# A two-layer graph network on one core: preparation in another order, and the edge network's first layer as one float32 product

## The chip, the cores and the metric

The kernel runs on one core of a Trainium2 chip. The metric is the device time of one execution in microseconds, as a median of several. Engines are named as in the profile: PE is TensorE (matmul) and PEld its weight load, DVE is VectorE, ACT ScalarE, POOL GpSimd, and SP SyncE, which only issues DMAs here.

## What is computed

The graph has 6250 nodes with 256 features and 100,000 edges sorted by target `dst`, each with 64 attributes. The reference, cut to what matters:

```python
h = relu(layernorm(x))
e = relu(edge_attr @ ee_w1 + ee_b1) @ ee_w2 + ee_b2        # edge network, 64 -> 256 -> 256
agg = segment_sum(h[src] + e, dst)                          # and a self edge for each node
h1 = (1 + eps) * h + agg
h1 = relu(ln(h1 @ w1 + b1)); h1 = relu(ln(h1 @ w2 + b2))    # 256 -> 1024 -> 1024
x = x + relu(ln(h + h1 @ w3 + b3))                          # 1024 -> 256
# then a graph attention layer (8 heads) over the same edges, added to x
```

## The kernel before

It runs in five stages, with a barrier between them.

**Preparation** (`prepare`). The nodes are 50 tiles of 125, taken in ten groups `c` of five. For a group, SyncE loads x; VectorE takes the statistics (`stats`: L315, L318 into `mv`); ScalarE takes the root (`deviation`, L241); VectorE makes the scale and offset (`coefficients`: L323, L324, the latter a product of `mv` and `rstd` on five columns); ScalarE normalises (L247); GpSimd adds a bias (L224, into `ht`) and clears half of the accumulator (L226); ScalarE rounds `ht` to float16 (`high`, L255) and VectorE subtracts to get the rest (`low`, L334); TensorE transposes both parts (L301, L302, into `own_ps`), and ScalarE and VectorE copy the transposed halves out (`own`, L261 and L329). Float32 values are kept throughout as a float16 high part and a float16 low part. The rows go to a table in DRAM. Besides, the kernel works out factors (`own_factors`), an offset by a small product (`own_offset`), and from `dst` a schedule of node tiles for each block of edges (`extremes`, `schedule`). Each engine has its own queue, written out in the loops over `c`; engines meet by semaphores.

**First edge stage** (`edges0`). 196 blocks of 512 edges. Per block GpSimd issues four indirect DMAs (L529), called gathers below, each of which fetches the table rows of 128 edges into `rows`, a ring of six blocks. SyncE loads the block's attributes, twice, into the two halves of `ea` (L493, L494). ScalarE rounds them to float16 (`high_parts`: `eab` L539, `eah` L540), VectorE subtracts for the low part (`low_parts`, L635). TensorE multiplies with the first-layer weights, which are split too: two float16 products for each of the four chunks of 128 edges (L583, L584). ScalarE takes the relu as high part (`rh`, L561), VectorE the low part (`rl`, L667). TensorE then sums rows and edge values by target with a one-hot matrix (`hot`, L407, made by VectorE): 32 products (L597, L598) for the block, and 32 more where it crosses into another tile. VectorE adds the sums to the accumulator (L644, L657). Twelve times in the stage a row of the dense weights is split as well (VectorE L719, L728). The ring is released by VectorE (L648).

**Dense stage** (`nodes`). The 50 tiles go through three layers in a software pipeline; `high_h` (ScalarE, L1120) and `low_h` (VectorE, L1183) split the next tile's input, `deviation(0)` and `inverse(0)` serve the first layer's normalisation.

**Second edge stage and end** (`edges1`, `finish`) do the attention over the same edges, with gathers of their own (L1538) and a float32 product for the sums (L1604).

Of the kernel before, what the change touches and what calls it, by code (L numbers as in the profile page):

```python
# [32 lines left out]
P = 128  # L33
# [23 lines left out]
def build(nc, t, out):  # L57

    with ExitStack() as ctx:
# [18 lines left out]
        with ExitStack() as first:  # L78
# [33 lines left out]
def prepare(nc, t, dram, sb):  # L112


    with ExitStack() as ctx:
# [20 lines left out]
        er = m.sb("er", [P, D], F32)  # L136
        ebr = m.sb("ebr", [ED + 2, D], F32)
        ebh = m.sb("ebh", [ED + 2, D], F16)
        stat = m.sb("stat", [TN, NT, 6], F32)
        mv = m.sb("mv", [TN, NT, 2], F32)  # L140
# [9 lines left out]
        own_ps = [[m.ps(f"own{s}{j}_ps", [P, 8, P]) for j in range(KD)] for s in range(2)]  # L150
        off_ps = own_ps[1][1][:, 7, 0:KD]
# [6 lines left out]
        eb_high, eb_split, ewb_done = m.sem("eb_high"), m.sem("eb_split"), m.sem("ewb_done")  # L158
# [19 lines left out]
        def _(sp):  # L178
# [4 lines left out]
            load_x(0)  # L183
            sp.dma_start(w2e[:], t["L0_gnn_ee_w2"].rearrange("(k p) n -> p k n", p=P)).then_inc(ld_w2e, 16)
            load_x(1)
            sp.dma_start(drow[:], t["dst_flat"].rearrange("(p j e) -> p j e", p=half, j=2)).then_inc(ld_dst, 16)
            for c in range(2, CH):
                load_x(c)
            sp.dma_start(sb["srcs"][:], t["src_cols"]).then_inc(stored, 16)
# [22 lines left out]
        def _(pool):  # L212
# [5 lines left out]
            pool.dma_start(sb["dsts"][:], t["dst_cols"]).then_inc(cols_in, 16)  # L218
            pool.wait_ge(ld_b2, 16)
            for c in range(CH):  # L220
# [5 lines left out]
                pool.memset(acc[:, tiles(c), D:2 * D], 0.0)  # L226
# [3 lines left out]
        def _(act):  # L230
# [3 lines left out]
            act.dma_start(er[0:ED, :], t["L0_gnn_ee_w1"]).then_inc(ld_small, 16)  # L234
            act.dma_start(er[ED:2 * ED, :], t["L0_gnn_ee_w1"]).then_inc(ld_small, 16)
            act.dma_start(ebr[0:ED, :], t["L0_gnn_ee_w1"]).then_inc(ld_small, 16)
            act.dma_start(ebr[ED:ED + 2, :], t["L0_gnn_ee_b1"].partition_broadcast(2)).then_inc(ld_small, 16)
# [19 lines left out]
            def own(c):  # L257
# [3 lines left out]
                act.activation(accT[:, tiles(c), 0, 0:TN], own_ps[c % 2][0][:, 0:PG, 0:TN], ACT.Identity,  # L261
                               bias=own_off[:, 0:1], scale=eps2[:]).then_inc(own_kept[0], 1)

            act.wait_ge(consts, 1)
            deviation(0)
            for c in range(CH + 3):
                if c < CH:
                    normalised(c)
                if c + 1 < CH:
                    deviation(c + 1)  # L270
                if c == 0:
                    act.wait_ge(ld_small, 16 * 4)
                    act.activation(sb["ewa"][:], er[:], ACT.Copy)
                    act.activation(ebh[:], ebr[:], ACT.Copy).then_inc(eb_high, 1)
# [4 lines left out]
                if c == 4:  # L279
                    act.wait_ge(eb_split, 1)  # L280
                    act.dma_start(sb["ewb"][ED:ED + 1, :], ebh[ED:ED + 1, :]).then_inc(ewb_done, 16)
            act.wait_ge(ewb_done, 16)

        @block.tensor
        def _(pe):
# [20 lines left out]
        def _(dve):  # L306
# [20 lines left out]
            def own(c):  # L327
                dve.wait_ge(own_done, c + 1)
                dve.tensor_scalar(accT[:, tiles(c), 1, 0:TN], own_ps[c % 2][1][:, 0:PG, 0:TN], eps2[:], own_off[:, 1:2],  # L329
# [46 lines left out]
            for c in range(CH + 3):  # L376
                if c < CH:
                    coefficients(c)
                if c + 1 < CH:
                    stats(c + 1)  # L380
# [1614 lines left out]
```

## Time and profile before

| | |
|---|---|
| median of 3 runs | 3149.57 us (3146.88 to 3150.08) |
| the profiled execution | 3146.9 us, span 3144.7 us |
| busy share of the span | PE 78%, PEld 69%, DVE 70%, ACT 47%, POOL 64% |
| DMA | 374.02 MB, mean 119 GB/s |

The shares are averages over stages that differ, so they don't say what bounds the kernel; the rows below are taken by stage. A matmul's duration includes the way through the array, so matmuls that follow each other overlap in the rows: how often they start says more than how long one is.

### The profile page before, as it was taken

Reading aid. Unit: us, or ns where it says so; the run is one execution under the profiler, and the core shown is the slowest. Engines: PE = TensorE matmul, PEld = TensorE weight load, DVE = VectorE, ACT = ScalarE, POOL = GpSimd, SP = SyncE. Lnnn points to the kernel's source line nnn. Section 1 sums busy time; section 2 is a strip of 40 time slices with the busy share of each in tenths; the row PEclk is TensorE's granted clock in tenths of the full one; section 3 lists DMA queues with packets and bytes.
Section 4 is the critical chain, followed back from the end, with each engine's and each line's share of the span. In section 5 each row is a group of like instructions: output and inputs, shape, how many; then the busy total and the mean of one; then the engine's idle time right before and its main releaser. Section 6 shows DMA issues by size and latency. Waiting matters only on the chain. (4 is left out here: it accounts for less than half of the span.)

```text
span 3144.7 us, 87336 instructions
## 1 busy us (share of the span) xinstructions
PE 2451.4 (78%) x29338; PEld 2168.6 (69%) x29339; DVE 2188.8 (70%) x3937; ACT 1481.8 (47%) x3763; POOL 2001.7 (64%) x2102
## 2 busy tenths in 40 slices
PE   2677777777777769999999999947777777777773
PEld 1566666666666669999999999935555555655552
DVE  7676667777676737777777777657667667666767
ACT  5444444444444448888888888831111111111114
POOL 4677777777777724444444444437777777777772
PEclk9998889999989989999999999979888878897886
DMA  6555555555555510000000000026555555555554
GB/s 157 167 159 150 157 158 160 162 162 162 160 162 158 152 29 20 20 21 20 23 20 21 20 23 20 21 73 176 172 168 173 173 173 168 172 173 174 171 168 139
DMA packets 184258, 374.02 MB, mean 119 GB/s; under 512 B 42757, under 2 KB 94103, under 8 KB 184184
## 3 DMA queue, kind: packets, MB, share of 16 engines
q0 software_dynamic: 75552, 209.66, 23.5%
q1 hardware_dynamic: 107664, 162.63, 17.3%
q10 hardware_dynamic: 968, 0.87, 0.1%
q8 instruction: 31, 0.51, 0.1%
q14 instruction: 43, 0.35, 0.0%
HBM read 347.21 MB, written 25.80 MB: 119 GB/s over the span
## 5 line engine op out<-in xcount | busy, mean ns | idle before, releaser
L529 POOL DMA_INDIRECT rows<-tab_scratch,srcs x784 | 770.5, 983 | 238.7 <-issue 234.4
L1538 POOL DMA_INDIRECT a_rows<-tab_scratch,srcs x784 | 751.6, 959 | 250.9 <-issue 232.2
L1604 PE MATMUL sum_ps<-feat,a_hot 128*125 128x264 f32 x1960 | 609.6, 468 | 229.5 <-DVE feat L1696 122.2
L1604 PEld LDWEIGHTS sum_ps<-feat,a_hot 128*125 128x125 f32 x1960 | 422.9, 225 | 335.5 <-DVE feat L1696 134.2
L951 PE MATMUL z_ps<-ah,w 128*128 128x125 f16 x6400 | 555.8, 219 | 0.7 <-PEq L1048 0.7
L951 PE MATMUL z_ps<-al,w 128*128 128x125 f16 x3200 | 544.8, 218 | 0.0
L951 PEld LDWEIGHTS z_ps<-ah,w 128*128 128x128 f16 x6400 | 491.5, 97 | 1.3 <-issue 1.3
L1548 ACT ACTIVATE feat<-d 128x32 f32<-128x32 f32 x196 | 44.9, 229 | 827.5 <-DVE d L1692 582.8
L597 PE MATMUL sum_ps<-hot,rows 128*128 128x125 f16 x1960 | 355.9, 235 | 41.9 <-DMA rows<-tab_scratch,srcs 20.9
L583 PE MATMUL mlp_ps<-ewa,eab 128*128 128x256 f16 x788 | 211.0, 298 | 226.8 <-PEq L579 222.3
L561 ACT ACTIVATE rh<-mlp_ps 128x1024 f16<-128x1024 f32 x196 | 199.6, 1018 | 346.4 <-ACTq L560 340.4
L914 POOL TENSOR_TENSOR a<-a 128x500 f32<-128x500 f32 x100 | 149.3, 1493 | 327.9 <-POOLq L913 327.9
L597 PE MATMUL sum_ps<-hot,rh 128*128 128x125 f16 x1960 | 353.9, 234 | 0.0
L598 PE MATMUL sum_ps<-hot,rows 128*128 128x125 f16 x1960 | 353.6, 234 | 0.0
L598 PE MATMUL sum_ps<-hot,rl 128*128 128x125 f16 x1960 | 353.5, 234 | 0.0
L1109 ACT ACTIVATE a<-z,pack 128x125 f32<-128x125 f32 x800 | 316.7, 487 | 39.5 <-ACTq L1107 39.5
L951 PEld LDWEIGHTS z_ps<-al,w 128*128 128x128 f16 x3200 | 315.9, 99 | 0.4
L667 DVE SCALAR_TENSOR_TENSOR rl<-mlp_ps,rh 128x1024 f16<-128x1024 f32 x196 | 240.0, 1225 | 48.2 <-DVEq L666 41.8
L583 PEld LDWEIGHTS mlp_ps<-ewa,eab 128*128 128x128 f16 x788 | 83.9, 106 | 261.5 <-issue 247.2
L597 PEld LDWEIGHTS sum_ps<-hot,rows 128*128 128x128 f16 x1960 | 205.9, 106 | 78.0 <-issue 46.2
L1083 ACT ACTIVATE z<-z_ps,pack 128x125 f32<-128x125 f32 x800 | 224.6, 366 | 38.8 <-ACTq L1081 38.8
L1696 DVE TENSOR_TENSOR feat<-a_rows,p_ps 128x1024 f32<-128x1024 f32 x196 | 239.2, 1220 | 3.9 <-DVEq L1484 0.5
(216 smaller groups left out, 5609.0 us busy)
## 6 DMA issues: line engine op xcount, KB each, us to landing
ea<-edge_t SPq DMA_DIRECT2D x394, 128.0 KB
dstb<-dst_flat SPq DMA_DIRECT2D x98, 512.0 KB
rows<-tab_scratch,srcs POOLq DMA_INDIRECT x784
a_rows<-tab_scratch,srcs POOLq DMA_INDIRECT x784
tab_scratch<-prow SPq DMA_DIRECT2D x50, 128.9 KB
hx<-x SPq DMA_DIRECT2D x50, 125.0 KB
x_scratch<-x SPq DMA_DIRECT2D x50, 125.0 KB
hs<-tab_scratch SPq DMA_DIRECT2D x50, 125.0 KB
```

The source lines that it names most:

```text
L529: pool.indirect_dma_start(rows[:, b % DEEP, k, :], None, dram["tab0"], bass.IndirectOffsetOnAxis(ap=srcs[:, c:c + 1], axis=0),).then_inc(r ...
L561: act.activation(rh[:, s].rearrange("p k d -> p (k d)"), mlp_ps[:, s].rearrange("p k d -> p (k d)"), ACT.Relu).then_inc(r_high, 1)
L583: pe.matmul(mlp_ps[:, s, k, :], eab[:, s, e], ewa[:], start=True, stop=False)
L597: pe.matmul(to, high, rhs, start=(k == 0 and q == 0), stop=False, skip_group_check=True)
L598: ins = pe.matmul(to, low, rhs, start=False, stop=(k == CB - 1), skip_group_check=True)
L667: dve.scalar_tensor_tensor(out=rl[:, s].rearrange("p k d -> p (k d)"), in0=mlp_ps[:, s].rearrange("p k d -> p (k d)"), scalar=0.0, in1=rh[ ...
L951: ins = pe.matmul(out, lhs, rhs, start=(k == 0 and q == 0), stop=(k == n - 1 and q == 2))
L1083: ins = act.activation(z[j][:, k, :], z_ps[j][:, half, (k % 4) * TN:(k % 4 + 1) * TN], ACT.Identity, bias=cols[b][:, k:k + 1], scale=(1.0, ...
L1109: ins = act.activation(a[j][:, k, :], z[j][:, k, :], ACT.Relu, bias=cols[be][:, k:k + 1], scale=cols[g][:, k:k + 1])
L1538: pool.indirect_dma_start(rows[:, b % DEEP, k, :], None, dram["tab1"], bass.IndirectOffsetOnAxis(ap=srcs[:, c:c + 1], axis=0),).then_inc(r ...
L1604: ins = pe.matmul(out[:], hot[:, h, k, :], feat[:, row, k, :], start=(k == 0), stop=(k == CB - 1))
L1696: return dve.tensor_tensor(feat[:, u, :, 0:D].rearrange("p k (h f) -> p k h f", h=HEADS), slot_of(slot)[:, :, 0:D].rearrange("p k (h f) -> ...
```

## The change

*Preparation.* `mv` moves to PSUM. `own_ps` has one buffer (two halves) instead of two, and TensorE now does all transposes of one half, then of the other, each behind the copy of the group before. GpSimd clears half the accumulator in two operations at the start. The table of ScalarE's root is asked for early by a one-element operation. Loads come in another order: x first, `dst` behind its third group, the second-layer weights behind its fifth, and the per-edge targets `dsts` later. The queues of VectorE and ScalarE are written in another order. The split of the first-layer weights goes.

*First edge stage.* The attributes are loaded once, with a row of ones below them, and multiplied as loaded with the float32 weights: one product for each chunk. `high_parts` and `low_parts` go. The product waits for the load itself; the slot of `ea` is released by ScalarE once the product is done.

*Dense stage.* `high_h` and `low_h` stand earlier in their queues, in front of `deviation(0)` and `inverse(0)`, and `row_deviation(1)` in front of `high_e`.

```diff
-                for name, shape, dt in [("ewa", [P, D], F16), ("ewb", [ED + 2, D], F16), ("dsts", [P, NCH + CB], F32)]:
+                for name, shape, dt in [("ew", [ED + 1, D], F32), ("dsts", [P, NCH + CB], F32)]:
...
-        mv = m.sb("mv", [TN, NT, 2], F32)
...
-        own_ps = [[m.ps(f"own{s}{j}_ps", [P, 8, P]) for j in range(KD)] for s in range(2)]
-        off_ps = own_ps[1][1][:, 7, 0:KD]
+        own_ps = [m.ps(f"own{j}_ps", [P, 8, P]) for j in range(KD)]
+        off_ps = own_ps[1][:, 7, 0:KD]
+        mv = m.ps("mv_ps", [TN, NT, 2])
+        spare = m.sb("p_spare", [1, 1], F32)
...
-            pool.dma_start(sb["dsts"][:], t["dst_cols"]).then_inc(cols_in, 16)
+            pool.memset(acc[:, 0:NT // 2, D:2 * D], 0.0)
+            pool.memset(acc[:, NT // 2:NT, D:2 * D], 0.0)
...
-                pool.memset(acc[:, tiles(c), D:2 * D], 0.0)
+                if c == 4:
+                    pool.dma_start(sb["dsts"][:], t["dst_cols"]).then_inc(cols_in, 16)
...
             act.wait_ge(consts, 1)
+            act.activation(spare[:], sb["lneps"][0:1, :], ACT.Sqrt)
             deviation(0)
...
-                if c >= 2:
-                    for j in range(KD):
-                        pe.wait_ge(own_kept[j], c - 1)
-                for k in range(PG):
-                    for j in range(KD):
-                        out = own_ps[c % 2][j][:, k, 0:TN]
+                for j in range(KD):
+                    if c:
+                        pe.wait_ge(own_kept[j], c)
+                    for k in range(PG):
+                        out = own_ps[j][:, k, 0:TN]
...
@@ def edges0(nc, t, dram, sb):
-        ea = m.sb("ea", [P, 2, BE], F32)
-        eab = m.sb("eab", [P, 2, BE], F16)
-        eah = m.sb("eah", [ED + 2, 2, BE], F16)
+        ea = m.sb("ea", [ED + 1, 2, BE], F32)
...
                 sp.dma_start(ea[0:ED, s, :], eb).then_inc(ea_ready[s], 16)
-                sp.dma_start(ea[ED:P, s, :], eb).then_inc(ea_ready[s], 16)
...
-                    high_parts(1 - s)
                     act.wait_ge(mlp_done, 1)
                     act.sem_inc(mlp_done, -1)
+                    act.sem_inc(ea_free, 1)
...
-                pe.wait_ge(ea_split, 1)
-                pe.sem_inc(ea_split, -1)
-                pe.sem_inc(ea_free, 1)
+                pe.wait_ge(ea_ready[s], 16)
+                pe.sem_inc(ea_ready[s], -16)
                 for k in range(CB):
-                    e = slice(k * P, (k + 1) * P)
-                    pe.matmul(mlp_ps[:, s, k, :], eab[:, s, e], ewa[:], start=True, stop=False)
-                    ins = pe.matmul(mlp_ps[:, s, k, :], eah[:, s, e], ewb[:], start=False, stop=True)
+                    ins = pe.matmul(mlp_ps[:, s, k, :], ea[:, s, k * P:(k + 1) * P], ew[:], start=True, stop=True)
                 ins.then_inc(mlp_done, 1)
...
-            def low_parts(s):
-                dve.wait_ge(ea_high, 2)
-                dve.sem_inc(ea_high, -2)
-                dve.tensor_tensor(eab[ED:P, s, :], ea[ED:P, s, :], eab[ED:P, s, :], ALU.subtract).then_inc(ea_split, 1)
...
                 with dve.Else():
-                    low_parts(1 - s)
                     low_activations(s)
                     add(1 - s, lo)
```

Two places show what this does to VectorE's queue. The first is preparation, in the middle of the ten groups: from one group's reciprocal to the next. Before:

```order
L323 RECIPROCAL rstd<-rstd 125x5
L324 SCALAR_TENSOR_TENSOR nmr<-mv,rstd 125x5
L315 BN_STATS stat<-acc 125x6 x5
L318 BN_AGGR mv<-stat 125x2 x5
L334 TENSOR_TENSOR tb<-ht,tb 125x5x256
L329 TENSOR_SCALAR acc<-own_ps,eps,own_off 128x5x125
```

And in the changed kernel:

```order
L313 RECIPROCAL rstd<-rstd 125x5
L314 SCALAR_TENSOR_TENSOR nmr<-mv_ps,rstd 125x5
L319 TENSOR_SCALAR acc<-own_ps,eps,own_off 128x5x125
L324 TENSOR_TENSOR tb<-ht,tb 125x5x256
L305 BN_STATS stat<-acc 125x6 x5
L308 BN_AGGR mv_ps<-stat 125x2 x5
```

The copy of an earlier group's transposes and the low part have moved in front of the next group's statistics, and the small product reads `mv_ps`.

The second place is the first edge stage, VectorE's branch for a block that stays in its tile. Before:

```order
L635 TENSOR_TENSOR eab<-ea,eab 64x512
L667 SCALAR_TENSOR_TENSOR rl<-mlp_ps,rh 128x1024
L644 ISA
L644 TENSOR_TENSOR acc<-acc,sum_ps 128x4x125
L407 ISA
L407 SCALAR_TENSOR_TENSOR hot<-dsts,negbase,e_iota_ps 128x500
```

And in the changed kernel:

```order
L631 SCALAR_TENSOR_TENSOR rl<-mlp_ps,rh 128x1024
L608 ISA
L608 TENSOR_TENSOR acc<-acc,sum_ps 128x4x125
L391 ISA
L391 SCALAR_TENSOR_TENSOR hot<-dsts,negbase,e_iota_ps 128x500
```

L635 has no successor; the rest stands as it stood.

## Rows read from the trace of the kernel before

**Rows 1.** Windows by stage: from:to, length, busy us (instructions) by engine, PEclk, DMA share, GB/s.

```profile
0.00:94.20 94.20, 24.62 (x208) 22.01 (x209) 69.74 (x163) 49.24 (x83) 41.73 (x31) 1.00 0.64 156
94.20:1114.00 1019.80, 750.30 (x9416) 663.61 (x9416) 716.03 (x923) 445.50 (x614) 771.41 (x785) 0.89 0.54 158
1114.00:2101.00 987.00, 932.73 (x14416) 920.91 (x14416) 674.88 (x1170) 807.28 (x2150) 436.28 (x502) 0.97 0.07 21
```

**Rows 2.** Sources L529 and L1538: ns min/median/max, first and last start; idle before.

```profile
L529 POOL DMA_INDIRECT rows<-tab_scratch,srcs x784: 952/957/1532, 95.3 to 1103.4; - x196
...
  issue: 234.4, 770
  DVEq L648: 4.3, 14
...
L1538 POOL DMA_INDIRECT a_rows<-tab_scratch,srcs x784: 944/946/1211, 2101.9 to 3091.8; - x196
```

**Rows 3.** Groups of instructions: busy us, mean ns of one, idle before.

```profile
L529 POOL DMA_INDIRECT rows<-tab_scratch,srcs x784 | 770.5, 983 | 238.7 <-issue 234.4 <-DVEq L648 4.3
...
L635 DVE TENSOR_TENSOR eab<-ea,eab 64x512 f16<-64x512 f32 x197 | 136.6, 693 | 130.7 <-DVEq L634 127.1
```

**Rows 4.** Timeline, first edge stage: start us, us, instruction, idle before.

```profile
496.23 0.69 DVE L635 TENSOR_TENSOR eab<-ea,eab 64x512 f16<-64x512 f32 x1
496.42 1.34 POOL L529 DMA_INDIRECT rows<-tab_scratch,srcs  x1 [0.30 <-issue]
496.95 1.23 DVE L667 SCALAR_TENSOR_TENSOR rl<-mlp_ps,rh 128x1024 f16<-128x1024 f32 x1
...
498.06 0.95 POOL L529 DMA_INDIRECT rows<-tab_scratch,srcs  x1 [0.30 <-issue]
```

**Rows 5.** Timeline, at the end of a weight row's split.

```profile
200.26 1.22 DVE L728 TENSOR_TENSOR w<-centred,w 128x1024 f32 x1
...
201.09 1.22 POOL L529 DMA_INDIRECT rows<-tab_scratch,srcs  x1 [0.30 <-issue]
```

**Rows 6.** Timeline of PE, first-layer products of one block.

```profile
501.60 0.27 PE L583 MATMUL mlp_ps<-ewa,eab 128*128 128x256 f16 x1 [1.33 <-PEq L579]
...
501.82 0.27 PE L583 MATMUL mlp_ps<-ewa,eab 128*128 128x256 f16 x1
```

**Rows 7.** Source L1604, second edge stage: ns min/median/max.

```profile
L1604 PE MATMUL sum_ps<-feat,a_hot x1960: 386/386/805, 2125.1 to 3102.6; 128*125 128x264 f32 x196
```

**Rows 8.** Window of L1604 alone: busy PE (matmuls touched), PEld, PEclk, DMA, GB/s.

```profile
2510.80:2512.00 1.20, 1.20 (x7) 1.03 (x6) 1.00 0.95 322
```

**Rows 9.** Timeline of preparation, one engine after the other.

```profile
44.61 0.18 DVE L323 RECIPROCAL rstd<-rstd 125x5 f32<-125x5 f32 x1
...
64.02 1.79 DVE L324 SCALAR_TENSOR_TENSOR nmr<-mv,rstd 125x5 f32<-125x5 f32 x1
65.73 1.72 DVE L315 BATCH_NORM_STATS2 stat<-acc 125x6 f32<-125x256 f32 x5
...
67.96 1.46 DVE L334 TENSOR_TENSOR tb<-ht,tb 125x1280 f16<-125x1280 f32 x1
...
77.85 0.18 DVE L323 RECIPROCAL rstd<-rstd 125x5 f32<-125x5 f32 x1
...
88.07 1.48 DVE L334 TENSOR_TENSOR tb<-ht,tb 125x1280 f16<-125x1280 f32 x1
...
92.08 0.93 DVE L329 TENSOR_SCALAR acc<-own_ps,eps,own_off 128x625 f32<-128x625 f32 x1 [1.26 <-PE own_ps L302]
...
65.85 2.56 ACT L247 ACTIVATE acc<-acc,nmr,rstd 125x256 f32<-125x256 f32 x5 [2.23 <-DVE nmr L324]
...
68.51 1.25 ACT L255 ACTIVATE tb<-ht 125x1280 f16<-125x1280 f32 x1
...
62.91 2.88 POOL L224 TENSOR_TENSOR ht<-acc,p_b2bc 125x1280 f32<-125x1280 f32 x1 [2.92 <-DVEq L336]
65.73 1.17 POOL L226 MEMSET acc<- 128x1280 f32 x1
```

**Rows 10.** Source L324: ns min/median/max, first and last start.

```profile
L324 DVE SCALAR_TENSOR_TENSOR nmr<-mv,rstd x10: 165/1418/1792, 13.3 to 78.2; 125x5 f32<-125x5 f32 x10
```

**Rows 11.** Waits of PE, 1240 to 1950 us: waited for, us in total, times, longest.

```profile
PE v_ps L981 <- PEq L980: 8.3, 38, 0.2
```

More of the change, by code:

```diff
@@ L181, in load_x @@
                     sp.dma_start(acc[rows, tiles(c), 0:D], x_v[rows, tiles(c), :]).then_inc(ld_x[c], 16)
[L183 to L187, printed above, removed]
+            for c in range(CH):
                 load_x(c)
+                if c == 2:
+                    sp.dma_start(drow[:], t["dst_flat"].rearrange("(p j e) -> p j e", p=half, j=2)).then_inc(ld_dst, 16)
+                if c == 4:
+                    sp.dma_start(w2e[:], t["L0_gnn_ee_w2"].rearrange("(k p) n -> p k n", p=P)).then_inc(ld_w2e, 16)
             sp.dma_start(sb["srcs"][:], t["src_cols"]).then_inc(stored, 16)
@@ L260, in own @@
                 act.wait_ge(own_done, c + 1)
-                act.activation(accT[:, tiles(c), 0, 0:TN], own_ps[c % 2][0][:, 0:PG, 0:TN], ACT.Identity,
+                act.activation(accT[:, tiles(c), 0, 0:TN], own_ps[0][:, 0:PG, 0:TN], ACT.Identity,
                                bias=own_off[:, 0:1], scale=eps2[:]).then_inc(own_kept[0], 1)
             act.wait_ge(consts, 1)
+            act.activation(spare[:], sb["lneps"][0:1, :], ACT.Sqrt)
             deviation(0)
@@ L268, in _ @@
                     normalised(c)
[L269 to L274, printed above, removed]
                 if 1 <= c < CH + 1:
@@ L278, in _ @@
                     own(c - 3)
[L279 to L282, printed above, removed]
+                if c + 1 < CH:
+                    deviation(c + 1)
+            act.wait_ge(ld_small, 16 * 2)
         @block.tensor
@@ L328, in own @@
                 dve.wait_ge(own_done, c + 1)
-                dve.tensor_scalar(accT[:, tiles(c), 1, 0:TN], own_ps[c % 2][1][:, 0:PG, 0:TN], eps2[:], own_off[:, 1:2],
+                dve.tensor_scalar(accT[:, tiles(c), 1, 0:TN], own_ps[1][:, 0:PG, 0:TN], eps2[:], own_off[:, 1:2],
                                   ALU.mult, ALU.add).then_inc(own_kept[1], 1)
@@ L378, in _ @@
                     coefficients(c)
+                if c >= 3:
+                    own(c - 3)
+                if 2 <= c < CH + 2:
+                    low(c - 2)
                 if c + 1 < CH:
                     stats(c + 1)
-                if c == 0:
+                if c < 2:
+                    extremes(c)
+                if c == 2:
                     own_factors()
-                if c == 1:
-                    extremes(0)
                     own_offset()
-                if 2 <= c < CH + 2:
-                    low(c - 2)
-                if c == 2:
-                    extremes(1)
-                    dve.wait_ge(eb_high, 1)
-                    settled(dve.tensor_tensor(sb["ewb"][:], ebr[:], ebh[:], ALU.subtract))
-                    dve.sem_inc(eb_split, 1)
-                if c == 3:
                     schedule()
-                if c >= 3:
-                    own(c - 3)
             for j in range(KD):
@@ L521, in _ @@
         def _(pool):
-            pool.memset(eah[ED:ED + 2, :, :], 1.0).then_inc(ones_ready, 1)
+            pool.memset(ea[ED:ED + 1, :, :], 1.0).then_inc(ones_ready, 1)
             for b in range(NB):
@@ L1148, in body @@
                     high(1, 0)
+                if has(i, 0, 1):
+                    high_h()
                 if has(i, 0):
@@ L1157, in body @@
                                    scale=sb["rstd0"][0:TN, bass.ds(i - 2, 1)]).then_inc(h0_ready, 1)
-                if has(i, 0, 1):
-                    high_h()
+                if has(i, 3):
+                    row_deviation(1)
                 if has(i, 0, 2):
                     high_e(i + 2)
-                if has(i, 3):
-                    row_deviation(1)
                 if has(i, 1):
@@ L1319, in body @@
                                                      op0=ALU.max, op1=ALU.add))
+                if has(i, 0, 1):
+                    low_h()
+                    dve.sem_inc(acc_free, 1)
                 if has(i, 0):
@@ L1337, in body @@
                     row_norm(1, h2[:], x1[:]).then_inc(h2_ready, 1)
-                if has(i, 0, 1):
-                    low_h()
-                    dve.sem_inc(acc_free, 1)
                 if has(i, 1):
```

24 lines of the change are left out of this document (4 added, 20 removed).

## The prediction

> **What bounds the kernel now.** I read the views in this order. First the busy time by stage [rows 1]: preparation 94.2 us, first edge stage 1019.8 us (94.2 to 1114), dense stage 987 us, and behind it the second edge stage and the end, which the diff does not touch. In the dense stage TensorE is busy 932.73 of 987 us, and what is missing lies in its first and last tiles. In the first edge stage no engine is: GpSimd 771 us, TensorE 750, VectorE 716, ScalarE 446. So I asked the gathers who they wait for [rows 2]. They wait for nobody: 770 of 784 have a gap of 0.30 us in front that the view calls "issue", and the 14 put down to L648 have the same 0.3 us (4.3 / 14). The gathers run back to back, from 95.3 to 1104.3 us, and this stream is the length of the stage; the others only have to keep up. The tail behind the last gather (about 10 us to 1114) is its landing, one block's sums and an add.
>
> The stream is not at its own pace, though. A gather's median is 957 ns and its mean 983 [rows 2, 3]: (983 - 957) x 784 = 20.4 us are lost in a few long ones. The timeline shows when [rows 4]: a gather issued while VectorE's L635 runs is 1.34 us long, that is 0.38 more than usual, and L635 had 0.50 us left to run at its start; the one issued beside L667 takes 0.95. I went through all 784: 102 start during an L635, with a mean of 1.141 us; 6 start during L728, and 5 of these are long, as the one of 1.22 us [rows 5]; the other 676 start beside nothing or beside L667, L644, L407, L657 or L719, and none of them is over 1.03 us. L635 and L728 are subtractions with both inputs in SBUF and a 16-bit result; the harmless large ones read PSUM.
>
> **The change, part by part.**
>
> *First edge stage, gathers.* L635 goes (197 of them), L728 stays (12). The 102 gathers gain 1.141 - 0.957 = 0.184 us each: **18.8 us**. What L728 costs, 20.4 - 18.8 = some 1.6 us, remains. No operation of the new VectorE order has two large SBUF inputs in its place. Bounds: nothing, if the long gathers have another cause; and 8.6 us more, (957 - 946) x 784, if the plain gather also falls to the 946 ns that it has in the second edge stage [rows 2], where less data moves beside it. I take neither: the 957 is the same beside every operation, so L635 isn't what makes it.
>
> *First edge stage, can the others still keep up?* The gathers' pace becomes 4 x 1.26 = 5.04 us a block. TensorE: eight products of a block become four. A pair's place is 501.82 - 501.60 = 0.22 us [rows 6]. The nearest row of a float32 product is L1604 in the second edge stage, 264 columns, 386 ns [rows 7]; at full granted clock seven of them touch a stretch of 1.20 us with the array busy throughout [rows 8], so they follow each other by about (1.20 + 0.386) / 7 = 0.23 us. For 256 columns that is 0.22 us: one float32 product takes the place of the pair, and TensorE's 750 us (3.83 a block) stay. ScalarE loses its two conversions of a block, VectorE 0.69 us [rows 3] of 3.65 (716 / 196), so both get slacker. TensorE no longer waits for VectorE's L635 in front of a block's first product; what it saves it will wait for gathers. New waits: the product waits for the attributes' DMA itself, and a slot is released by ScalarE behind the product, about 0.9 us later than now. Its load has to land before the product after next; the sums of a block and another product lie between, over 3 us, and SyncE issues one load where it issued two. In the present order no long DMA wait stands in front of the reader. If one did, the sums behind it on TensorE's queue would wait too, but only GpSimd's ring of six blocks (30 us) would turn that into time. I cost all this at nothing; the cover is 5.04 - 3.83 = 1.2 us a block.
>
> *Preparation.* From group 4 to group 9 of five tiles each, VectorE's reciprocals L323 stand at 44.61 and 77.85 us, 6.65 a group [rows 9]. Its chain in a group: L324 at 64.02, statistics from 65.73, low part from 67.96 to 69.4, then a wait for TensorE and the copy L329. L324 works on five columns yet takes 1.79 us: it ends with GpSimd's addition of 62.91 to 65.79; its shortest is 0.165 [rows 10]. With the mean in PSUM it should not be held, as L329 (one PSUM input) never is. That takes up to 1.6 us out of each group. Against it stands the single buffer: the transposes of a group wait until the last ones are copied out by both engines, and both copies wait for the transposes. I walked the new queues with the durations of [rows 9]: on ScalarE 2.6 normalise, 1.25 high part, 0.9 copy; on VectorE 2.2 statistics, 1.46 + 0.3 low part, 0.93 copy; on TensorE 2.1 for a group; 0.1 for a semaphore. The opening memsets (ten times 1.17 us, from 1.6 to 13.3 us) may hold VectorE's casts, so group 0 has its coefficients at 14.2 us. Then group 1 at 18.4, group 2 at 23.1, group 3 at 33.3 (factors, offset and schedule now all stand in front of it), group 4 at 39.1 against 44.6 (its schedule was held by GpSimd), then steps of 5.7 and 7 us in turn, and group 9 at 71.5 against 77.9. The tail gives part of it back. Now all low parts come early, the last at 88.07 and its copy at 92.08 [rows 9]; then transposes (2.1), copy (0.9) and next low part (1.8) are in series, 4.8 us for each of the last three groups. The walk ends its last copy at 89.5 instead of 93.0: **3.5 us** saved. Bounds: 8 us if the tail overlaps after all; 4 us lost if L324 is still held (1.6 for each of five groups, less the slack that the single buffer leaves).
>
> *Dense stage.* ScalarE rounds h and VectorE subtracts it one operation earlier, before the deviation and the reciprocal of layer 1. TensorE needs them only a layer later, and its only steady wait is 8.3 us in 38 pieces of 0.2 [rows 11]. Moving 0.43 us in front of a chain that ends in activations for which TensorE has several us of layer-2 work costs nothing; at most 1 us either way in the first tiles. **0.**
>
> Sum: 18.8 + 3.5 + 0 = 22.3 us. The profiled execution took 3146.9 us (span 3144.7), the lowest of the three runs; their median is 3149.57. From the profiled one the sum gives 3124.6, from the median 3127.3. I say **3126 us**, -0.7%. A measurement of this kernel can't tell 0.2% (6.3 us) from no change.
>
> **The rivals.**
> 1. *The gathers' delay isn't L635's.* The issue of a gather would be long for a reason of its own, and only preparation is left: 3149.6 - 3.5 = 3146, no change that can be measured. Against it: 65 long gathers, all inside two lines. The Trainium skill, page "SBUF — State Buffer", section "Who interferes with whom", speaks for this rival: a probe found that a tensor_copy stalls such DMAs but tensor_tensor does not, because making descriptors needs the write interface. By that rule the sum would be 3.5 us. The rows here disagree with it, [rows 4] by 0.38 us in one gather. Chance 6%.
> 2. *The float32 product is dearer than the pair, and TensorE becomes the bound* (the slower side). The cover of 1.2 us a block is 0.30 for each of four products, so this decides from a place of 0.52 us on, where the pair's is 0.22. At twice the place, 0.44, a block needs 3.83 + 0.88 = 4.7 us, still under 5.04; but 3.83 holds at the mean granted clock of 0.89 [rows 1], and if it fell to 0.80 a block would need 4.7 x 0.89 / 0.80 = 5.23, 196 x 0.19 = 37 us above the gathers' pace: about 3163. For it: the granted clock does fall in this stage, and a mean hides where. Against: [rows 8], and a TensorE that falls behind has no idle time. The Trainium skill, page "FP8 and Floating Point Precision", section "TensorE Precision Notes", has four passes for true FP32. By it 256 columns would take 0.43 us at 2.4 GHz; [rows 8] shows about two passes. Chance 4%.
> 3. *The plain gather gets faster too*, toward 946 ns, as 25 MB of loads go: 3126 - 8.6 = 3117. Chance 10%.
> 4. *Preparation gets longer*, L324 still held: +4 instead of -3.5, the rest as forecast: 3133. Chance 8%.
>
> **How the numbers follow.** Forecast 72%, rivals 6, 4, 10 and 8. The range goes from rival 3 to rival 4: 3116 to 3134, which leaves out rivals 1 and 2, the ends of 3 and 4, and a drift of the baseline by 3 us. Faster by over 0.2%: forecast, 3 and 4, less a little, 0.91; within 0.2%: rival 1 and part of 2, 0.06; slower 0.03.
>
> **What the changed kernel's profile would show.** Gathers: median 957, mean about 960, long ones only beside the weight rows' subtraction; first to last start 989 us instead of 1008. First-layer products: four of about 386 ns a block, 0.22 apart at full clock. More of TensorE's idle time put down to the rows' DMA, none to VectorE in front of the product. Preparation: the small L324 operation 0.17 us each, last copy near 89.5, first gather near 92 (now 95.3). Dense stage 987 us. The prediction is wrong if gathers are long beside another operation, if GpSimd waits for free rows by more than its 0.3 us, or if the opening memsets hold VectorE past 14 us.

## The result and the profile after

The changed kernel is slower: 3174.93 us (median of 5 runs, 3172.25 to 3188.62) against 3149.39, a ratio of 1.0091 with a 95% interval from 1.0076 to 1.0105. The prediction was 3126 us and faster. The profiled execution took 3172.9 us, with a span of 3171.1 where before has 3144.7. A kernel's time is the median of its executions; one of the seven of `k17_old_dense` took 5221 us, and its ratio leaves that one out. Where the 26.4 us of the two spans lie follows from a few moments of the two traces: the first gather, the last gather, the first instruction of the dense stage (SyncE's load of w2e), the first gather of the second edge stage, and the end:

| | before | after | |
|---|---|---|---|
| preparation, to the first gather | 95.3 | 93.8 | -1.5 |
| first to last gather of the first edge stage | 1008.1 | 1022.4 | +14.3 |
| last gather to the dense stage | 10.7 | 18.2 | +7.5 |
| dense stage | 987.8 | 985.9 | -1.9 |
| first gather of the second edge stage to the end | 1042.8 | 1050.7 | +7.9 |

The windows of the stages, beside [rows 1] (busy us of PE, PEld, DVE, ACT, POOL, then PEclk, DMA share, GB/s):

```profile
0.00:92.80 92.80, 24.48 (x208) 22.04 (x209) 56.31 (x162) 49.24 (x82) 41.34 (x23) 1.00 0.65 157
92.80:1134.40 1041.60, 903.16 (x9416) 819.02 (x9416) 574.62 (x726) 225.84 (x220) 754.44 (x785) 0.89 0.44 130
1134.40:2120.00 985.60, 936.02 (x14416) 924.08 (x14416) 680.42 (x1171) 797.36 (x2151) 418.26 (x502) 0.97 0.07 21
```

In the first edge stage TensorE went from 750 to 903 us of work, on the same 9416 records. VectorE and ScalarE lost 141 and 220 us. The gathers, beside [rows 2]:

```profile
L508 POOL DMA_INDIRECT rows<-tab_scratch,srcs x784: 947/953/1991, 93.8 to 1116.2; - x196
its engine sat idle before it (us, times) until:
  issue: 230.3, 756
  DVEq L612: 39.6, 28
```

Two things are to be seen. Their mean is 961 ns (753.6 / 784): of before's 65 long ones nine are left, of 1.2 to 2.0 us, each beside the subtraction of a weight row (L688). But 28 gathers now wait for L612, VectorE's release of the ring: 39.6 us, where the 0.3 us of issue would make 8.4. So they wait some 31 us for those who use the rows. And the first-layer products, as a source:

```profile
L553 PE MATMUL mlp_ps<-ew,ea x1576: 379/379/767, 96.3 to 1131.0; 65*128 65x256 f32 x197
its engine sat idle before it (us, times) until:
  issue: 103.6, 34
  PEq L551: 97.8, 33
```

The page has them and the sums as groups (busy us, mean ns of one, idle before). PEq is TensorE's own queue, which stood at the line named:

```profile
L553 PE MATMUL mlp_ps<-ew,ea 65*128 65x256 f32 x1576 | 426.2, 418 | 97.8 <-PEq L551 97.8
L566 PE MATMUL sum_ps<-hot,rows 128*128 128x125 f16 x1960 | 356.2, 235 | 41.5 <-PEq L582 25.5
```

The code issues 197 x 4 = 788 products and the trace has 1576: a float32 product is two matmul records of 379 ns each. The timeline of TensorE shows what a block's four cost, once behind a wait and once in a dense stretch:

```profile
528.14 0.22 PE L567 MATMUL sum_ps<-hot,rl 128*128 128x125 f16 x1
531.21 3.23 PE L553 MATMUL mlp_ps<-ew,ea 65*128 65x256 f32 x8 [2.85 <-PEq L551]
...
1077.36 1.95 PE L553 MATMUL mlp_ps<-ew,ea 65*128 65x256 f32 x8
1079.14 0.22 PE L566 MATMUL sum_ps<-hot,rows 128*128 128x125 f16 x1
```

At full clock the sums start 1.78 us behind the first product (1079.14 - 1077.36), which is 0.44 us for each of four, twice the pair's 0.22 [rows 6]. Behind a wait of 2.85 us the same four take 3.23 us. The windows of both places differ in the granted clock (the column behind POOL's), 0.59, which is mostly the lower level of 1.2 GHz, against 1.00:

```profile
531.20:534.40 3.20, 3.19 (x10) 2.40 (x11) 0.00 (x0) 0.00 (x0) 2.28 (x4) 0.59 0.30 92
1077.40:1079.20 1.80, 1.80 (x12) 1.50 (x10) 1.04 (x2) 0.00 (x0) 1.36 (x2) 1.00 0.25 75
```

Such a wait stands in front of L553 33 times, 97.8 us in all: once at the stage's start (5.6 us) and then at every sixth block, once a turn of TensorE's own loop. With the start-up, TensorE so needs 903.2 + 97.8 = 1001.0 us for itself, 5.11 us a block. A stage whose gathers wait for nobody would take as long: before's 1019.8 us less the 18.8 of the forecast. So TensorE has no slack left and has become the bound. What is still missing of the 1041.6 us are 41.5 us in front of the sums, in 25 pieces. Nine of these are 2.2 to 4.4 us long, 30 us together, and each ends some 5 us behind the start of VectorE's reduction of a weight row (L679), when the low part or the one-hot matrix comes late.

### The profile page after: what moved, and what is told of

It is laid out like the page before. It is cut to its first block and busy times, and to the rows that moved or that the text cites. A ratio compares the mean times of both kernels' runs of the same rounds, so it can differ in the third digit from the quotient of the medians.

```text
span 3171.1 us, 85946 instructions
## 1 busy us (share of the span) xinstructions
PE 2603.2 (82%) x29338; PEld 2320.9 (73%) x29339; DVE 2037.0 (64%) x3739; ACT 1252.1 (39%) x3368; POOL 1973.2 (62%) x2094
## 5 line engine op out<-in xcount | busy, mean ns | idle before, releaser
L508 POOL DMA_INDIRECT rows<-tab_scratch,srcs x784 | 753.6, 961 | 269.9 <-issue 230.3
L1564 PE MATMUL sum_ps<-feat,a_hot 128*125 128x264 f32 x1960 | 598.3, 460 | 240.8 <-DVE feat L1656 116.6
L1564 PEld LDWEIGHTS sum_ps<-feat,a_hot 128*125 128x125 f32 x1960 | 413.8, 221 | 346.7 <-issue 134.4
L553 PE MATMUL mlp_ps<-ew,ea 65*128 65x256 f32 x1576 | 426.2, 418 | 97.8 <-PEq L551 97.8
L553 PEld LDWEIGHTS mlp_ps<-ew,ea 65*128 65x128 f32 x1576 | 309.3, 207 | 142.4 <-issue 103.6
L566 PE MATMUL sum_ps<-hot,rows 128*128 128x125 f16 x1960 | 356.2, 235 | 41.5 <-PEq L582 25.5
```

The costliest lines, as they stand in the source:

```text
L508: pool.indirect_dma_start(rows[:, b % DEEP, k, :], None, dram["tab0"], bass.IndirectOffsetOnAxis(ap=srcs[:, c:c + 1], axis=0),).then_inc(r ...
L553: ins = pe.matmul(mlp_ps[:, s, k, :], ea[:, s, k * P:(k + 1) * P], ew[:], start=True, stop=True)
L566: pe.matmul(to, high, rhs, start=(k == 0 and q == 0), stop=False, skip_group_check=True)
L1564: ins = pe.matmul(out[:], hot[:, h, k, :], feat[:, row, k, :], start=(k == 0), stop=(k == CB - 1))
```

## The experiments

By theory A the product's doubled place (the time for which it holds the array) costs the time, because TensorE then is the bound. By theory B it is the product's new wait for the load, or the slot's later release, and by theory C the new preparation or dense stage. Theory A1 came later and says why 0.88 us a block, less than the prediction's cover of 1.2, was enough. A single time in round brackets is before's median in the same runs.

**1. Which part costs it.** `k1_pair_back` is the changed kernel with `edges0` and the weight split of before; `k2_f32_only` is before with only this:

```diff
-                    pe.matmul(mlp_ps[:, s, k, :], eab[:, s, e], ewa[:], start=True, stop=False)
-                    ins = pe.matmul(mlp_ps[:, s, k, :], eah[:, s, e], ewb[:], start=False, stop=True)
+                    ins = pe.matmul(mlp_ps[:, s, k, :], ea[:, s, k * P:(k + 1) * P], ew[:], start=True, stop=True)
```

> The changed kernel with the first layer of before (two float16 products, both conversions, both loads) and its split weights put back; the new preparation and the new dense stage stay. Theory A (the float32 product takes 0.44 us of TensorE where the pair takes 0.22, and that alone costs the time): the first edge stage is as before, first to last gather 1008 us with 102 long ones, and the total is 3149.5 less what preparation saved in the changed kernel (1.5 us), 3146 to 3149. Theory B (the new wait for the load, with a slot of the attributes released later, costs the time): the same, since this goes too. Theory C (the reordered preparation or dense stage costs it): it stays near 3170.

> The kernel before with the first layer of the changed one and nothing else; preparation and dense stage as before. Theory A: the whole loss is here, 3172 to 3177, with first to last gather near 1022 us, GpSimd waiting for free rows by some 30 us, and a last block that is summed 16 to 25 us behind its gathers instead of 4 to 12. Theory B gives the same. Theory C: 3126 to 3130, the stage shorter by the 18.8 us of the gathers.

Measured: 3145.95 us with the pair back and 3172.87 with the float32 layer alone (3149.7), ratios 0.999 [0.998, 1.0] and 1.0075 [1.0058, 1.0092]. The loss is the first layer's, and theory C falls.

**2. The load's wait or TensorE's time.** `k4_three_slots` gives the attributes a third slot, so each load has a block's time more (SyncE's loop is written out for it):

```diff
-        ea = m.sb("ea", [ED + 1, 2, BE], F32)
+        ea = m.sb("ea", [ED + 1, 3, BE], F32)
...
-            sp.sem_inc(ea_free, 1)
+            sp.sem_inc(ea_free, 2)
```

`k3_high_only` rounds attributes and weights to float16 and makes one float16 product a chunk; `k5_high_x2` and `k5_high_x4` make it two and four times:

```diff
-                    ins = pe.matmul(mlp_ps[:, s, k, :], ea[:, s, k * P:(k + 1) * P], ew[:], start=True, stop=True)
+                    for _ in range(4):
+                        ins = pe.matmul(mlp_ps[:, s, k, :], eah[:, s, k * P:(k + 1) * P], ewh[:], start=True, stop=True)
```

`k8_bf16_x4` makes four as well, but on the attributes where they were loaded (the upper halves, read as bfloat16), with the changed kernel's wait and release.

> The changed kernel with three slots of attributes instead of two, so that each load has a whole block's time more to land. Theory A: the same within 0.1%, 3170 to 3177, with the same waits for free rows. Theory B: most of the loss goes, 3130 to 3155, and the idle time of TensorE in front of the first-layer product falls.

> The changed kernel with the attributes and the weights rounded to float16 by ScalarE and one float16 product a chunk; the low parts of attributes, weights and bias are left out of the computation. There is no subtraction beside the gathers, and TensorE has 0.44 us a block less than in before. Theory A: the gathers run at their own pace, first to last start 988 to 990 us, no wait for free rows, the last block summed within 12 us of its gathers, total 3120 to 3128. Theory B (the load's landing and release): here ScalarE waits for the load and TensorE releases the slot as before, so it also expects a fast kernel; the two are told apart by the kernel with three slots.

> The kernel with the one float16 product of high parts, each product made twice into the same place (low parts still left out): TensorE has 0.22 us a chunk, the place that the prediction gave to the float32 product, and everything else as in the kernel with one. Theory A says that this is what the prediction really forecast: first to last gather 988 to 992 us, total 3124 to 3134. If TensorE were already the bound at the pair's price, it is 10 us or more above the kernel with one product (3129).

> The same with each float16 product made four times: 0.44 us a chunk on TensorE, as the float32 product, but with the load waited for by ScalarE and released by TensorE as in before. Theory A (TensorE's time alone): 3166 to 3178, with waits for free rows and a late last block as in the changed kernel. Theory B (the load's wait and late release, or the float32 operands themselves): near the kernel with one product, 3125 to 3140. Between the two is what the float32 product costs besides its time.

> The changed kernel with TensorE still waiting for the load itself and ScalarE still releasing the slot, but the product made as four 16-bit ones, reading the upper halves of the attributes as bfloat16 where they lie, with weights rounded to bfloat16 once (the low parts are left out of the computation). If only TensorE's time counts, it equals the run with four float16 products behind ScalarE's conversion (3161.7): 3157 to 3167. If the new wait and the late release cost something of their own, it is at the changed kernel's 3175.

| kernel | place of a chunk's product, us | median, us | ratio and interval | first to last gather, profiled execution |
|---|---|---|---|---|
| k4_three_slots | 0.44 | 3176.71 | 1.0089 [1.0072, 1.0106] | 1024.5 |
| k3_high_only | 0.11 | 3129.16 | 0.9931 [0.9915, 0.9948] | 989.0 |
| k5_high_x2 | 0.22 | 3128.89 | 0.9937 [0.992, 0.9953] | 990.6 |
| k5_high_x4 | 0.44 | 3161.66 | 1.0032 [1.0019, 1.0044] | 1017.1 |
| k8_bf16_x4 | 0.44 | 3152.06 | 1.0006 [0.9995, 1.0016] | 1002.2 |

(Places worked out from counts and the float16 place of [rows 6], half a pair.) A third slot changes nothing. Between one and two float16 products nothing changes either, and four cost 33 us: a threshold, not a slope. `k5_high_x2` is the kernel that the prediction described, at the place it had assumed, and it takes 3128.9. Its gathers wait for nobody. Theory A holds for these 33 of the 46 us between `k5_high_x2` and the changed kernel. Theory B falls: with the changed kernel's own wait and release, four 16-bit products (`k8_bf16_x4`) are not slower than `k5_high_x4`, but 10 us faster.

`k3_high_only` came out 1 us above its range. Both runs with four products came out below what was expected of them, 3166 to 3178 and 3157 to 3167. In part this is the float32 product itself: the first-layer products keep TensorE busy for 426.2 us in the changed kernel, 417.4 in `k5_high_x4` and 412.8 in `k8_bf16_x4`, which is 2.16, 2.12 and 2.10 us a block (1.20 in before). The 8.8 us to `k5_high_x4` are most of the 13 between their medians. Between the two runs with four products some 4 us lie in the dense stage, where the granted clock stood at its lower level for 10.2 us of the weight products in `k5_high_x4` and never in `k8_bf16_x4`; the rest is open.

**3. Who lengthens the gathers.** The pair stays, but the subtraction reads its first input from a copy in PSUM, which ScalarE puts where the block's product will land:

```diff
+                act.wait_ge(mlp_free, 1)
+                act.sem_inc(mlp_free, -1)
+                act.activation(copy_ps(s), ea[ED:P, s, :], ACT.Copy).then_inc(ea_high, 1)
...
-                dve.tensor_tensor(eab[ED:P, s, :], ea[ED:P, s, :], eab[ED:P, s, :], ALU.subtract).then_inc(ea_split, 1)
+                dve.tensor_tensor(eab[ED:P, s, :], copy_ps(s), eab[ED:P, s, :], ALU.subtract).then_inc(ea_split, 1)
```

> The kernel before, with the float16 pair kept; ScalarE also copies the second half of the attributes (64 x 512, float32) into the part of mlp_ps that the block's own product will overwrite, and L635's subtraction reads that copy instead of the one in SBUF, so that it has one input in SBUF and one in PSUM. If the lengthened gathers come from its two SBUF inputs, first to last gather falls from 1008 to 988 to 992 us and the total to 3128 to 3134. If they come from the operation being a subtraction, its size or its 16-bit result, nothing changes: 3147 to 3152. If ScalarE's further operation makes the others late: above 3155.

> The same first layer (float16 pair, subtraction reading PSUM) with the new preparation and the new dense stage. If preparation is worth the 1.5 to 4 us that the run with the pair put back showed: 3125 to 3130, the fastest of all.

Measured: 3159.5 and 3157.81 us (3151.14), 1.0032 and 1.0027. Two groups of lines of `k6_copy_in_psum`, and the wait of its new operation:

```profile
L533 POOL DMA_INDIRECT rows<-tab_scratch,srcs x784 | 753.6, 961 | 254.7 <-issue 232.6 <-DVEq L657 22.1
...
L644 DVE TENSOR_TENSOR eab<-mlp_ps,eab 64x512 f16<-64x512 f32 x197 | 136.7, 694 | 193.3 <-DVEq L643 189.4 <-ACT mlp_ps L546 2.0
...
L546 ACT ACTIVATE mlp_ps<-ea 64x512 f32<-64x512 f32 x197 | 117.5, 597 | 307.6 <-ACTq L545 300.0 <-issue 6.4
```

The subtraction is as frequent, as large and as long as before (694 ns), its result is the same 16-bit one, and the gathers' mean fell from 983 [rows 3] to 961. 82 gathers start while it runs, with a mean of 0.956 us and none over 0.960, where 102 had 1.141. So it is its two inputs in SBUF that lengthen them. The gain was lost again, and both forecasts (3128 to 3134, 3125 to 3130) were missed. ScalarE stands 300 us in front of the copy, with a relu queued behind it, the gathers wait 22.1 us for free rows where before had 4.3, and TensorE's first product of the dense stage comes 28 us behind the last gather instead of 20. Moving the copy behind the relu, and the subtraction behind VectorE's low part, was meant to end that:

> The kernel with the float16 pair and the subtraction reading a copy in PSUM, with the copy moved behind ScalarE's relu of the block before and the subtraction behind VectorE's low part of that block, so that neither relu nor low part stands behind the wait for the free place in mlp_ps (in the first form ScalarE stood 299 us there). Expected: first to last gather 988 to 995 us and 3126 to 3138 in all, against 3159.5 of the first form. If the product now waits for the later subtraction: the gathers as short as that, but waits for free rows remain and the total is above 3145.

> The same first layer with the new preparation and dense stage: 2 to 4 us below the kernel with the copy moved, 3123 to 3135.

It made things far worse: 3296.84 and 3293.75 us (3148.57). By the code, product, relu, low part, subtraction and the next product now each wait for the one before, and the trace fits this: TensorE waits in front of 195 of its 197 blocks of products, 381.5 us.

**4. What took the cover.** By the prediction's own sum, 0.88 us more a block left 3.83 + 0.88 = 4.7 under 5.04. Theory A1: the waits of 3.0 us, one in each turn of TensorE's loop, are its own and are no cover; 97.8 / 196 = 0.50 us a block, and 4.7 + 0.50 = 5.2 is over 5.04. Before has these waits too; two, six blocks apart, in its timeline:

```profile
602.15 0.37 PE L583 MATMUL mlp_ps<-ewa,eab 128*128 128x256 f16 x1 [3.17 <-PEq L579]
...
636.79 0.37 PE L583 MATMUL mlp_ps<-ewa,eab 128*128 128x256 f16 x1 [3.04 <-PEq L579]
```

`k11_turns_of_12` and `k12_before_turns_of_12` put twelve blocks into a turn, in the changed kernel and in before:

```diff
-            with pe.Fori(0, FULL) as i:
-                tiles = tiles_of(nc, PE, table, DEEP * i, DEEP)
+            with pe.Fori(0, FULL // 2) as i:
+                for v in range(2):
+                    tiles = tiles_of(nc, PE, table, 2 * DEEP * i + DEEP * v, DEEP)
```

> The changed kernel with TensorE's loop over blocks holding twelve blocks a turn instead of six (the six blocks' tile numbers are still read ahead of each six), so that it turns 16 times instead of 32; nothing else. In the changed kernel TensorE idles 33 times for about 3.0 us in front of a first-layer product, once a turn, 97.8 us in all, which is 0.50 us a block. Theory A1 (this wait takes the cover away: 4.7 us of products and sums a block plus 0.50 is 5.2, over the gathers' 5.04) and the wait belongs to the loop's branch: 16 waits go, 48 us of TensorE's time, it keeps up again with the gathers, and the total is 3126 to 3140. If the wait belongs to the reading of the tile numbers: 33 waits as before and 3170 to 3178, no news on A1. Theory A2 (the wait is only slack, TensorE's products alone are the bound): waits go but the time stays above 3165.

> The kernel before with the same twelve-block turns of TensorE's loop. There the gathers set the pace with or without the wait, so theory A1 expects no change: 3145 to 3153 where before has 3149 to 3151, first to last gather 1008 us. A gain of over 8 us would say that the wait costs time in itself and not by using up the cover.

Measured: 3244.81 and 3196.93 us (3148.57), 1.0306 [1.0289, 1.0323] and 1.0159 [1.014, 1.0178]. Neither was foreseen, so these two runs don't decide on A1. The timeline of `k11_turns_of_12`, in the middle of a turn and at its end:

```profile
486.00 3.40 PE L553 MATMUL mlp_ps<-ew,ea 65*128 65x256 f32 x8 [2.72 <-PEq L551]
...
527.74 3.75 PE L553 MATMUL mlp_ps<-ew,ea 65*128 65x256 f32 x8 [8.15 <-PEq L551]
```

The queue that loads instructions, on the page of `k11_turns_of_12` (packets, MB, share) and then on the changed kernel's, which here reads as before's:

```profile
q8 instruction: 170, 2.79, 0.4%
```

```profile
q8 instruction: 31, 0.51, 0.1%
```

In the middle of a turn, with no branch of the loop, 2.7 us: that is the reading of twelve tile numbers (six first tiles and six ends). At the end of a turn it is 5.4 us more here and 3.3 to 6.4 in the others, while code is loaded again: the 139 further packets are about nine a turn, and two or three of these start within 6 us of a turn's end. Twelve blocks are too long to stay; in a turn of six the code stays, and the 3.0 us are almost all reading. The Trainium skill, page "Runtime: NRT & Kernel Launch", section "Instruction fetch mechanics", gives some 200 ns for a register loaded from memory; an estimate from it is 2.4 us for twelve, and the 2.7 us here agree roughly. The same section of the Trainium skill says that a jump out of the loaded part must fetch its target; the 170 packets agree. So the wait can be shortened where the reading is:

```diff
                 edge_mlp(1 - s)
+                if u == 0:
+                    tiles.extend(tiles_of(nc, PE, table, DEEP * i, DEEP if i is not FULL else REST))
                 lo, end = tiles[u]
...
-                tiles = tiles_of(nc, PE, table, DEEP * i, DEEP)
+                tiles = []
```

`k13_read_behind_product` is the changed kernel with this, `k15_before_read_behind` is before with it, and `k14_read_split` is as `k13_read_behind_product` but reads the six ends behind the block's first sums.

> The changed kernel with one edit on TensorE's queue: the reading of the six blocks' tile numbers, which stands at the head of a turn, comes behind the issue of the turn's first first-layer product, so that the product (1.95 us) runs meanwhile. Theory A1 (2.6 us of the 3.0 are the reading, and these 3.0 us a turn are what used up the cover): the wait in front of the product nearly goes, one of some 0.7 to 1 us appears in front of the sums, TensorE needs 5.20 - 0.3 to 0.4 = 4.8 to 4.9 us a block, under the gathers' 5.04; waits for free rows go and the total is 3126 to 3140. Theory A2 (products alone are the bound): above 3165.

> The same with the reading in two: the first tiles behind the product, the ends behind the block's first 32 sums. If each part hides behind its own work, the idle time per turn falls under 0.5 us and the total is 0 to 5 us below the kernel with both behind the product; if the second part stands in the open (1.3 us, since the sums' queue is empty by then), it is 0 to 8 us above it.

> The kernel before with the same edit as k13 (reading behind the product). The gathers set its pace and TensorE's idle time is not its bound, so theory A1 expects 3145 to 3153, no change against before. A gain of more than 8 us would say that the 3.0 us cost time in both kernels, not as lost cover.

Measured: 3131.79 us (0.9938 [0.9921, 0.9955]), 3132.70 (0.9941 [0.9924, 0.9958]) and 3153.64 (1.0007 [0.9997, 1.0017]), beside 3150.6. Sources of `k13_read_behind_product`, its product and its gathers:

```profile
L553 PE MATMUL mlp_ps<-ew,ea x1576: 378/379/766, 96.0 to 1084.9; 65*128 65x256 f32 x197
its engine sat idle before it (us, times) until:
  issue: 5.8, 1
  PEq L551: 5.6, 1
...
L508 POOL DMA_INDIRECT rows<-tab_scratch,srcs x784: 949/953/1990, 93.6 to 1083.8; - x196
...
  DVEq L614: 5.2, 17
```

And its timeline at the head of a turn:

```profile
554.00 0.22 PE L567 MATMUL sum_ps<-hot,rl 128*128 128x125 f16 x1
554.06 1.95 PE L553 MATMUL mlp_ps<-ew,ea 65*128 65x256 f32 x8
557.64 0.23 PE L566 MATMUL sum_ps<-hot,rows 128*128 128x125 f16 x1 [1.64 <-PEq L584]
```

The product is as dear as in the changed kernel (379 ns a record). The wait of 3 us is gone from in front of it, and 1.6 stand behind it. At the median of the turns 2.99 us have become 1.75, so 1.2 us of idle time are given back. The product at the head of a turn, with no wait in front, now mostly runs at the full clock: its four take 2.03 us in the mean of the heads instead of 2.87. (The two effects came by one edit, and no run parts them.) The gathers wait for nobody again (17 x 0.3 us), 990.2 us from first to last, though the weight rows are split as they were. One moved read is worth 43 us in the changed kernel and no gain in before (3 us more, with an interval that includes 1), where the gathers set the pace. That is what A1 expected, and A2, by which the products alone are the bound (above 3165), falls. Reading in two parts brings nothing more.

**5. Preparation and dense stage apart**, on the kernel just found: `k16_old_preparation` has before's preparation (without the weight split) and the new dense stage, `k17_old_dense` the reverse.

> k13 (float32 product, tile numbers read behind it; 3131.8) with the old preparation and the new dense stage. The dense stage from first to last weight product is 912 to 918 us if the shorter stage comes from its own reordering (then its term was -5 instead of 0), 921 if not. If the slower gathers of the second edge stage come with the new preparation, they have 946 ns here, those of the first stage 957, and the total is 3126 to 3131 (7 us less there, 3 more in the first stage, 1.5 more in preparation); if with the new dense stage, 957, and the total is 3131 to 3137.

> k13 with the new preparation and the old dense stage: the complement. Dense stage 921 us if its reordering is what shortens it; gathers of the second edge stage 957 ns if they follow the preparation (total 3135 to 3139), 946 if they follow the dense stage (3128 to 3132).

Measured: 3126.51 us (0.993 [0.9913, 0.9946]) and 3136.91 (0.9961 [0.9949, 0.9973]), beside 3150.21. Sources of the gathers of the second edge stage and of the dense stage's weight products, of the first and then of the second kernel:

```profile
L1500 POOL DMA_INDIRECT a_rows<-tab_scratch,srcs x784: 944/946/1216, 2082.0 to 3072.5; - x196
L913 PE MATMUL z_ps<-ah,w x6400: 215/219/313, 1128.5 to 2043.6; 128*128 128x125 f16 x194
```

```profile
L1500 POOL DMA_INDIRECT a_rows<-tab_scratch,srcs x784: 952/957/1247, 2084.7 to 3081.7; - x196
L913 PE MATMUL z_ps<-ah,w x6400: 216/219/313, 1125.6 to 2046.3; 128*128 128x125 f16 x194
```

From first to last weight product it is 915.1 us with the new order and 920.7 with the old. The other traces agree: 920.7 to 922.4 with the old order in all kernels, 911.8 to 918.3 with the new, and there the longer ones are those in which the granted clock fell to its lower level meanwhile (for 10.2 us in the changed kernel's 918.3, never in the 911.8 of `k1_pair_back`). The gathers of a stage that nobody touched take 946 ns with the old preparation and 957 with the new. `k16_old_preparation` is the fastest kernel of all, 0.7% under before.

## Why the prediction was wrong

- **The step that failed is the float32 product's place**, put at 0.22 us: "one float32 product takes the place of the pair", so that TensorE's 750 us would stay. It measured 0.44, and TensorE's work in the stage became 903 us. The step read [rows 7, 8] as one record for one product. The count stood in the same row: 196 blocks and 49 further tiles, four products each, make 980, and the row has 1960. The seven matmuls in 1.20 us were three and a half products. The Trainium skill, page "FP8 and Floating Point Precision", section "TensorE Precision Notes", says four passes, and the trace agrees (four times the 0.11 us of a float16 product); the sentence in the prediction that saw two passes was a miscount.
- **The cover was mis-sized too.** "5.04 - 3.83 = 1.2 us a block" set TensorE's busy time against the gathers' pace and left out its own waits. They can be found in before's trace: in front of the product of every sixth block stands one of 2.4 to 3.2 us, or a longer one that covers it (2.1 and 1.7 at the first and the last turn). With 0.50 off, the cover was 0.7 us a block and rival 2 decided from a place of 0.22 + 0.7 / 4 = 0.40, not 0.52. By the prediction's threshold of 0.52 even the right price of 0.44 would have passed. With only one of the two the kernel is faster than before, as `k5_high_x2` (place 0.22) and `k13_read_behind_product` (place 0.44, shorter wait) show.
- **Rival 2 is what happened**, at 3175 instead of 3163, through these waits and the slow product behind them, and not by the lower mean clock that it was priced with (0.89 in the stage, as in before). It had 4%. GpSimd waiting for free rows, one of the signs named for being wrong, is what the trace shows.
- **The gathers' delay was right.** `k6_copy_in_psum` names its cause as two inputs in SBUF, against rival 1 and against the rule of the Trainium skill that is quoted there. The mean fell to 961 ns where 960 was forecast, and a stream whose consumers keep up runs in 989 to 994 us (forecast 989). The last nanosecond of it is luck: the nine long gathers that stay cost 6.5 us and not 1.6, while the median is 953 and not 957, which is worth 3.
- **The reason given for a faster plain gather (rival 3) was misread.** The 946 ns of the second edge stage were put down to less data moving there; before's trace has 170 GB/s in that stage and 158 in the first [rows 1]. And the median doesn't fall with the loads: `k2_f32_only`, with 26 MB less and the old preparation, keeps 957, and `k1_pair_back`, with all loads and the new preparation, has 953.
- **Preparation**: the PSUM mean freed the small product (0.16 us for all ten, forecast 0.17), the steps and the tail of 4.8 us a group came as walked, but the walk was 2 us too early at group 4 already (41.2 us, forecast 39.1). The last copy ended at 91.6 instead of 89.5, and 1.5 us were saved where 3.5 were forecast. What was not forecast is the 6 to 8 us more that the second edge stage takes with it.
- **The dense stage**, costed at 0, is 5.6 us shorter in `k16_old_preparation` than in `k17_old_dense`; of this the changed kernel kept 3.1 us (918.3 against before's 921.4, by the weight products).
- **The chances** don't add up as they stand: forecast, rival 3 and rival 4 make 0.90, not 0.91.

## What to carry to other kernels

Before a duration is used as a price, divide the trace's count by the number of operations in the code: one operation can be several records. An engine's need is its busy time plus the idle time that it makes itself, and only waits for others are cover; sort its waits by what they recur with (here every sixth block, the turn of its own loop). When a consumer is near the bound, put register reads behind issued work: the same change was 25 us slower or 19 us faster by the place of one read.

## What was unexpected of the hardware

- A float32 matmul of 65 x 256 shows as two records of 379 ns and holds the array for 0.44 us at full clock, four float16 ones.
- Reading twelve tile numbers into registers holds TensorE's queue for 2.3 to 2.9 us, and the product behind such a wait ran at a granted clock of 0.59 (3.2 us instead of 1.95).
- A loop body of twelve blocks instead of six adds some 5.4 us to each turn and takes the instruction queue from 31 to 170 packets.
- A VectorE subtraction with both inputs in SBUF lengthens an indirect DMA that GpSimd issues beside it (1.141 us in the mean), and the same one with an input in PSUM does not (0.956).
- Indirect DMAs of one program are uniformly slower than those of another that has the same code for them: 946 to 947 ns or 957 at the median in the second edge stage, by which preparation had run, in all the kernels here. In the first edge stage it is the other way, 957 with the old preparation and 953 or 954 with the new. Why is open.
